# A one-core attention-plus-experts block: transposed inputs from the host, a row region per expert, a gathered return, and every engine's program written out

## The reference, cut to what matters

```python
x = x + attn(layernorm(x))        # 16 heads of 8 features, no softmax
    q, k = l2norm(x @ Wq + bq), l2norm(x @ Wk + bk);  v = x @ Wv + bv
    out  = (q @ k.T) / n ** sigmoid(m) @ v;  return out @ Wo + bo
h = layernorm(x)
    logits = h @ router_w.T       # 16 experts, top 1 for each row
    score  = sigmoid(top logit);  gate, up = split((h * score) @ gate_up[e])
    routed = (up * silu(gate)) @ down[e]
    shared = silu(h @ shared_gate.T) * (h @ shared_up.T) @ shared_down.T
return x + shared + routed
```

## Time and profile before

| | us |
|---|---|
| median of 3 runs | 277.24 (275.02 to 279.43) |
| the profiled execution, its own time | 278.11 |
| its span in the trace | 276.1 |
| busy: PE, PEld, DVE, ACT, POOL | 197.2, 169.9, 146.3, 102.3, 139.2 |
| the chain that ended last, by engine | DMA 25%, issue 20%, PE 16%, POOL 16%, DVE 15%, ACT 3% |
| of that: returning scatter (DMA and POOL) | 13% and 9% |
| of that: forward scatter (DMA and POOL) | 9% and 3% |

### The profile page before, as it was taken

How to read it: one execution, slowest core, us unless ns; L and a number is a source line. 1 busy time by engine, 2 the same in 40 slices (tenths; PEclk the granted TensorE clock), 3 DMA queues, 4 the chain that set the end, 5 groups by cost and what they waited for, 6 DMA issues and landing times.

```text
span 276.1 us, 3634 instructions
## 1 busy us (share of the span) xinstructions
PE 197.2 (71%) x1195; PEld 169.9 (62%) x1195; DVE 146.3 (53%) x368; ACT 102.3 (37%) x198; POOL 139.2 (50%) x148
## 2 busy tenths in 40 slices
PE   1786988798777699479999600999999999910000
PEld 1346666577577588468888500999999888810000
DVE  2269799999962866962333300476776333300041
ACT  3314548577574763702222100345554422200000
POOL 8004754667666130655555652014657666667360
PEclk9996899999987956959999955799999999995555
DMA  4998020250000000001111113234430111111396
GB/s 122 286 375 290 34 76 2 67 165 1 0 4 0 0 0 2 1 29 48 42 38 42 44 47 96 63 93 118 133 98 39 49 48 50 48 39 48 122 305 209
DMA packets 27906, 22.59 MB, mean 82 GB/s; under 512 B 2401, under 2 KB 24945, under 8 KB 27889
## 3 DMA queue, kind: packets, MB, share of 16 engines
q1 hardware_dynamic: 22640, 15.85, 19.9%
q0 software_dynamic: 2560, 5.26, 5.3%
q10 hardware_dynamic: 2688, 1.25, 1.6%
HBM read 11.83 MB, written 10.53 MB: 81 GB/s over the span
## 4 chain that ended last, share of the span: by engine, by line
DMA 25%; issue 20%; PE 16%; POOL 16%; DVE 15%; ACT 3%; SPq 1%; POOLq 0%; DVEq 0%; ACTq 0%
DMA y_rows<-yg,home 13%; DMA x_slots<-h_rows,pos 9%; POOL y_rows L438 9%; POOL x_slots L429 3%; DVE qkv L656 3%; DVE st L621 2%; DMA h_rows<-y_rows 2%; PE quad_banks L891 2%; DVE ss L665 2%; PE bank L975 1%; SPq L326 1%; PE bank L902 1%; PE bank L881 1%; DVE ss L669 1%; PE quad_banks L935 1%
## 5 line engine op out<-in xcount | busy, mean ns | idle before, releaser
L438 POOL DMA_INDIRECT y_rows<-yg,home x48 | 45.9, 957 | 43.6 <-DMA y_rows<-yg,home 20.5
L700 DVE TENSOR_TENSOR s_act<-quad_banks,sg_act 128x512 f32<-128x512 f32 x32 | 22.0, 691 | 44.3 <-PE bank L975 37.8
L429 POOL DMA_INDIRECT x_slots<-h_rows,pos x32 | 30.8, 963 | 22.2 <-DMA x_slots<-h_rows,pos 9.5
L531 ACT ACTIVATE sg_act<-quad_banks 128x512 f32<-128x512 f32 x32 | 18.9, 597 | 56.1 <-PE quad_banks L937 56.1
L975 PEld LDWEIGHTS bank<-sdT,s_act 128*128 128x128 f32 x256 | 35.7, 205 | 2.9
L975 PE MATMUL bank<-sdT,s_act 128*128 128x128 f32 x256 | 35.8, 288 | 0.0
L375 POOL TENSOR_TENSOR qkv<-qkv,rn 128x512 f32<-128x512 f32 x16 | 16.9, 1076 | 33.0 <-DVE rn L673 33.0
L891 PE MATMUL quad_banks<-w_c,xT 128*128 128x384 f32 x64 | 25.3, 543 | 1.7 <-ACT xT L480 1.2
L935 PE MATMUL quad_banks<-hT,sgT 128*128 128x512 f32 x32 | 16.3, 510 | 5.2 <-DVE s_act L700 5.2
L891 PEld LDWEIGHTS quad_banks<-w_c,xT 128*128 128x128 f32 x64 | 13.0, 214 | 11.1 <-issue 2.4
L1060 PE MATMUL bank<-ident,xg 128*128 128x128 f32 x48 | 7.7, 287 | 16.1 <-DMA xg<-x_slots 16.0
(11 more groups left out here) (146 smaller groups left out, 487.3 us busy)
## 6 DMA issues: line engine op xcount, KB each, us to landing
x_slots<-w_raw SPq DMA_DIRECT2D x8, 387.0 KB, 6.2
xg<-x_slots SPq DMA_DIRECT2D x12, 258.0 KB, 2.8
xres<-L_attn_x SPq DMA_DIRECT2D x8, 256.0 KB, 5.7
w_raw<-L_ffn_gate_up_proj SPq DMA_DIRECT2D x4, 512.0 KB, 3.6
h_rows<-y_rows SPq DMA_DIRECT2D x8, 256.0 KB, 5.2
out<-xres ACTq DMA_DIRECT2D x4, 256.0 KB, 4.7
out<-xres SPq DMA_DIRECT2D x4, 256.0 KB, 4.5
y_rows<-yg,home POOLq DMA_INDIRECT x48, 2.2
```

The costliest lines, as they stand in the source:

```text
L429: g.indirect_dma_start(out=x_slots, out_offset=bass.IndirectOffsetOnAxis(ap=pos[:, t:t + 1], axis=0), in_=h_rows[:, t, :], in_offset=None) ...
L438: g.indirect_dma_start(out=y_rows, out_offset=bass.IndirectOffsetOnAxis(ap=home[:, n:n + 1], axis=0), in_=yg[:, n, :], in_offset=None).the ...
L531: a.activation(sg_act[:, k % 2], pair[:, 2 * (k % 2)], ACT.Silu).then_inc(s_silu, 1)
L700: v.tensor_tensor(s_act[:, k % 2], pair[:, 2 * (k % 2) + 1], sg_act[:, k % 2], ALU.mult).then_inc(s_act_rdy, 1)
```

## The change

The whole program is written anew. What it does:

- **The host** passes x a second time in features-first form (`x_t`), stores x and the output in the layout of the SBUF tile (2 KB pieces for each partition and chunk), and passes a centering matrix, the joined q, k and v weights and biases, and every FFN weight already turned. The turns of x and of weights on PE are gone, with their copies.
- **Bias and residual** go into PSUM by PE (`attend`: an fp32r product of 512 columns, and a float32 product of the identity by 512 columns of x), and ACT copies the sum out. `add_bo` on POOL and `add_attn` on DVE are gone.
- **Router and experts' gate and up** use one plain float32 product instead of three fp32r ones; the experts' weights are no longer split. The shared products keep their split.
- **A region for each expert**: `x_slots` has 16 regions of 4096 + 128 rows. Ranks count within the expert alone, so a chunk's rows are placed as soon as the chunk is routed. Every chunk has its own `choose`, `count`, `count_before` and `place`, and the 32 scatters of POOL stand inside attention. The first 128 rows of each region are zeros, and an expert's last tile is filled up with them.
- **The score** is no longer put on the rows. The rows carry their top logit as a 129th column, and the sigmoid (silu of the logit over the logit) is applied in the expert stage, as a scale.
- **Loads**: a table of the first row of each of the 48 tiles is computed after the last chunk; SP reads it into registers and issues 48 loads of 128 rows (12 x 4).
- **Return**: each group is stored by SP in slot order (`y_slots`), and after all stores have landed POOL issues 32 indirect DMAs that gather the rows of each tile into SBUF. The adds follow chunk by chunk.
- **Every engine's list** is written out call by call, with the wait of each PE call as an argument.

The shape of the additions in the diff (the order lists and helpers cut to a few lines each):

```diff
-    x_slots = nc.dram_tensor("x_slots", (SLOTS, W), F32, kind="Internal").ap()
-    y_rows = nc.dram_tensor("y_rows", (1 + T + SLOTS, D), F32, kind="Internal").ap()
+    x_slots = nc.dram_tensor("x_slots", (E * REG, W), F32, kind="Internal").ap()
+    y_slots = nc.dram_tensor("y_slots", (SLOTS * P, D), F32, kind="Internal").ap()
...
+            def load(g):
+                first = slot_values(0, g, mybir.EngineType.SP, E * REG - P)
+                if g == 0:
+                    sp.wait_ge(zero_st, 16)
+                    for landed in scat:
+                        sp.wait_ge(landed, 16 * NT // 2)
+                for j in range(Q):
+                    sp.dma_start(xg[:, g * Q + j, :], x_slots[bass.ds(first[j], P), :]).then_inc(xg_ld[g], 16)
...
+            for stored in y_st:
+                pool.wait_ge(stored, 16 * NG // YRING)
+            pool.wait_ge(y_row_rdy, 1)
+            for t in range(NT):
+                if t >= 2:
+                    pool.wait_ge(back[t % 2], 16 * (t // 2))
+                g.indirect_dma_start(out=h_rows[:, t, 0:D], out_offset=None, in_=y_slots,
...
+            def take_y(g):
+                act.wait_ge(e_dn_mm, g + 1)
+                if g >= YRING:
+                    act.wait_ge(y_st[g % YRING], 16 * (g // YRING))
...
+            def choose(c):
+                dve.wait_ge(log_mm, c + 1)
+                logits = log_bank(c)[:, 0:Q * E].rearrange("p (t e) -> p t e", e=E)
+                top = h_rows[:, Q * c:Q * c + Q, D]
+                link(v.tensor_reduce(top, logits, AX.X, ALU.max))
+                link(v.tensor_tensor(far[:], logits, top.unsqueeze(2).broadcast_to([P, Q, E]), ALU.is_lt))
...
+            def place(c):
+                dve.wait_ge(base_mm, c + 1)
+                base = log_bank(c)[:, 128:128 + E]
+                link(v.tensor_tensor(offs[:], incl[:, c % 2], base.unsqueeze(2).broadcast_to([P, E, Q]), ALU.add))
+                link(v.tensor_tensor(offs[:], offs[:], hot[:, c], ALU.mult))
+                link(v.tensor_reduce(rank[:], offs[:].rearrange("p e t -> p t e"), AX.X, ALU.add))
+                v.tensor_tensor(pos[:, Q * c:Q * c + Q], rank[:], near[:], ALU.add).then_inc(pos_rdy, 1)
...
+                te.matmul(ps_qy[:], ones_r[:], bo_two[:].rearrange("p j d -> p (j d)"), start=True, stop=False)
+                te.matmul(ps_qy[:], ident[:], xres[:, Q * c:Q * c + Q, :].rearrange("p j d -> p (j d)"), start=False,
+                          stop=False)
...
+                    mm = te.matmul(gate_up_banks(g % 2)[:, j, :], xgT[:, g % 2, P * j:P * j + P],
+                                   gu_cols[:, bass.ds(held[g][j] * 2, F2)], start=True, stop=True)
```

More of the change, by code:

```diff
@@ L427, in _, with scatter @@
+            def scatter(t):
+                if t % Q == 0:
+                    pool.wait_ge(pos_rdy, t // Q + 1)
                 if t >= 2:
@@ new lines, in _ @@
+            scatter(0)
+            scatter(1)
+            hT_lo(1)
+            scatter(2)
+            scatter(3)
+            scale_v(4)
+            scale_q(4)
+            count(1)
+            scale_v(5)
+            scale_q(5)
+            scatter(4)
+            scatter(5)
+            scatter(6)
+            count(2)
+            scatter(7)
+            hT_lo(2)
+            scatter(8)
+            scatter(9)
+            hT_lo(3)
+            scatter(10)
+            scatter(11)
+            count(3)
@@ new lines, in _ @@
+            scale_v(6)
+            scale_q(6)
+            scatter(12)
+            scatter(13)
+            scale_v(7)
+            scatter(14)
+            scatter(15)
+            scale_q(7)
+            scatter(16)
+            scatter(17)
+            count(4)
+            hT_lo(4)
+            scatter(18)
+            scatter(19)
+            count(5)
+            hT_lo(5)
+            scatter(20)
+            scatter(21)
+            hT_lo(6)
+            scatter(22)
+            scatter(23)
@@ L706, in _ @@
+            v.memset(zeros[:], 0.0).then_inc(z_done, 1)
             dve.wait_ge(ach, 1)
@@ L854, in _ @@
-            shared(0, C1)
-            over_groups(experts, dve, lambda k: act_shared(C1, k))
-            shared(C1, NQ)
-            add_experts(NQ - 1)
+            x_stats(2)
+            x_scales(1)
+            take(0, 0)
+            x_stats(3)
+            take(0, 1)
+            bias_rows()
+            take(1, 0)
+            x_stats(4)
+            head_sums(0)
+            take(1, 1)
+            scale_mask()
+            inv_norms(0)
+            x_stats(5)
+            head_sums(1)
@@ new lines, in _ @@
+            head_sums(3)
+            inv_norms(3)
+            x1_stats(1)
+            take(4, 0)
+            choose(0)
+            mask_vk(1)
+            h_scales(1)
+            take(4, 1)
+            place(0)
+            take(5, 0)
+            head_sums(4)
+            take(5, 1)
+            inv_norms(4)
+            x1_stats(2)
+            head_sums(5)
+            choose(1)
+            inv_norms(5)
+            h_scales(2)
+            x1_stats(3)
+            place(1)
+            take(6, 0)
@@ new lines, in _ @@
+            h_scales(3)
+            mask_vk(2)
+            take(6, 1)
+            choose(2)
+            take(7, 0)
+            head_sums(6)
+            place(2)
+            x1_stats(4)
+            take(7, 1)
+            h_scales(4)
+            inv_norms(6)
+            choose(3)
+            head_sums(7)
+            x1_stats(5)
+            place(3)
+            act_shared(0)
+            inv_norms(7)
+            choose(4)
+            h_scales(5)
+            act_shared(1)
+            place(4)
@@ new lines, in _ @@
+            mask_vk(3)
+            x1_stats(6)
+            choose(5)
+            h_scales(6)
+            place(5)
+            x1_stats(7)
+            h_scales(7)
+            choose(6)
+            place(6)
+            act_shared(2)
+            choose(7)
+            place(7)
+            act_shared(3)
+            act_shared(4)
+            slot_rows()
+            act_shared(5)
+            take_table()
+            y_rows()
+            act_shared(6)
+            add_shared(0)
+            act_shared(7)
@@ L961, in gate_up_shared, with turn_h @@
-            def gate_up_shared(c, k):
-                n = c * KC + k
-                if not (isinstance(c, int) and n < 2):
-                    pe.wait_ge(s_act_rdy, n - 1)
-                h = hT[:, :, bass.ds(c * 512, 512)]
+            def turn_h(c, after=None):
+                pe.wait_ge(h_rdy, c + 1)
+                free(after)
+                for j, t in enumerate(tiles(c)):
+                    last = te.transpose(ps_hT[:, P * j:P * j + P], h_rows[:, t, 0:D], ident[:])
+                last.then_inc(hT_mm, 1)
```

1581 lines of the change are left out of this document (921 added, 660 removed).

## The result

The changed kernel takes 241.24 us (median of 4 runs, 238.15 to 242.28), where the kernel before took 277.85 on the same chip (4 runs, 275.02 to 279.43). The ratio is 0.867, with a 95% interval of 0.859 to 0.875: clearly faster. The forecast was 234.0, range 219 to 252. The profiled execution took 240.65 us, its span is 238.7. Some executions of one and the same kernel run slower, at a lower granted clock; the ratios and intervals here leave them out.

| event (us from the span's start) | predicted | measured |
|---|---|---|
| first take on DVE | 10.5 | 12.35 |
| last `place` | 98 | 112.8 |
| last forward scatter landed | 112 | 121.1 |
| rows at PE | 116 | 125.8 |
| last expert group done | 170 | 180.5 |

The account below looks back on a forecast made before the run. DVE was taken to bound attention, and POOL's indirect DMAs to keep PE waiting afterwards. Last `place` at 98, rows at PE 116, last group 170, gathers to 226 gave a span of 232.8 and 234 us, range 219 to 252.

Parts of the forecast that it names:

- Step 1: Kernel start: DVE's first take moves from 14.31 to about 10.5 us, a gain of 4 us.
- Step 2: Attention: 82.7 us of DVE work at density 0.93 takes 89 us; last `place` done at 98.
- The warning row L787: Attention: DVE instructions with two SBUF inputs held by POOL, 37 us if always, 5 us expected.
- Step 3: Forward scatters in POOL's list: 44 us taken for 32, landed at 112, rows at PE at 116.
- (a): Attention: POOL and DVE hold each other, landing waits +6 us, held instructions +10: 250 us; chance 0.17.
- Step 4: Expert stage: 3.51 us of PE for each of twelve groups, plain product 1.83; last group done at 170.
- Step 5: Return: last store landed at 174, 32 gathers 1.57 us apart to 226, span 232.8.
- (b): Return: gathers land in 3 us for 2.3, about 2.1 apart, +17 us: 251 us; chance 0.1.
- (c): SP's queue: 48 loads at 1 us each delay the stores, +12 us: 246 us; chance 0.06.
- (d): End: gathers 1.26 us apart, so PE's shared units set the end: 221 us; chance 0.13.
- (e): Return: slower than before, 283 us, if gathers wait serially by twos at 3.1 us apart; chance 0.02.
- Its own signs: Right: DVE over 18 of 20 us busy, 20 to 90; wrong: DVE instructions of 0.9 beside POOL's, DVE under 80%.

Follow-up runs that it names:

- late_scatter: The kernel after, with the 32 forward scatters moved behind the last count in POOL's list: 274.44 us, ratio 0.987.
- engines_cleared: The kernel after, with the first four shared products moved behind the last route and throwaway PE work in attention instead: 242.54 us, ratio 0.878.
- gather_four: The kernel after, with four returning gathers in flight instead of two: 232.69 us, ratio 0.838.
- shared_behind: The kernel after, with shared gate-and-up products 11 to 13 and down products 11 and 12 moved behind the last expert group: 240.39 us, ratio 0.868.
- four_behind: The kernel after, with four gathers and four scatters in flight and shared products 11 to 13 behind the last expert group: 234.79 us, ratio 0.846.
- all_three: four_behind, with the experts' gate and up product also taken once from rounded rows and weights: 227.55 us, ratio 0.824.
- one_product_b: The kernel after, with the experts' gate and up product taken once from rounded rows and weights, rounded by POOL: 235.33 us, ratio 0.847.

## Why the prediction was right, and where it was off

**The direction and the bulk of the size** were right for the stated reason. Taking the scatters out of attention again cost 33 us in `late_scatter`, and the two stages of the earlier trace rows in which PE waited for POOL are filled. That the sum came within 3% is in part luck: 14.8 us too few up to the last `place` met 5.7 too many for the scatters and 5.3 too many for the return. A slip of 0.2 us in the last addition (226, 0.8 and 5.8 are 232.6) changes nothing.

**Step 1, start.** The first take came at 12.35, a gain of 2 us for 4. DVE's list has statistics of three chunks and two scales ahead of the take, and the second of them waited for x to land (DVE, kernel after):

```profile
9.75 0.87 DVE L694 BATCH_NORM_STATS2 st<-xres 128x6 f32<-128x128 f32 x4 [3.04 <-DMA xres<-L_attn_x]
...
12.35 1.11 DVE L731 SCALAR_TENSOR_TENSOR qkv<-quad_banks,rs,b_qkv 128x384 f32<-128x384 f32 x2
```

From 9.75 to 12.35 DVE hardly paused, so the landing of x and the statistics set the start.

**Step 2, the last `place` at 98, is the step that failed in size:** 112.8. The split of DVE's own time shows where. Busy time of DVE in the kernel after, to the 4.01 us wait and from there to the last `place`:

```profile
0.00:87.90 87.90, 76.01 (x246) 0.98 0.42 123
87.90:112.90 25.00, 13.35 (x51) 0.73 0.10 32
```

The sum had 82.7 us of work; it was 76.01 + 13.35 = 89.4, 6.7 more. The ten small instructions took 25.4 us for the 17.2 assumed (the records overlap a little, so their sum is more than they add to the 89.4): unheld they are 0.16 to 0.30 us, 18.5 for 80, and the rest is L765, L780 and L782 being held. Idle time ahead of 87.9 was 11.9 us; by the prediction's 4 us and its density, for the work that it had ahead of the tail, it would have been 9.2: 2.7 more. And the tail of 25.0 us would by the density of 0.93 and the 5 us for the last chunk's chain have been 13.35/0.93 + 5 = 19.4: 5.6 more. 6.7 + 2.7 + 5.6 = 15.0, the whole miss. A density read from the full pipeline was used to its very end, where the pipeline drains: there is one chain and not eight. Some 2.5 of the tail's 25 us are shared work on PE at the lower clock (`engines_cleared`); the rest of its idle time is the waits of the chain.

**The warning row L787 was read rightly, its price was too low.** A held instruction ends with the tensor instruction of POOL that stands beside it (DVE and POOL of the kernel after):

```profile
56.26 1.69 DVE L765 SCALAR_TENSOR_TENSOR far<-far,place_of 128x64 f32<-128x64 f32 x1
...
72.82 1.53 DVE L717 SCALAR_TENSOR_TENSOR nm<-mv,rs 128x4 f32<-128x4 f32 x1
```

```profile
55.74 2.11 POOL L308 TENSOR_TENSOR qkv<-qkv,rn 128x512 f32<-128x512 f32 x2
...
73.03 1.29 POOL L318 TENSOR_TENSOR hT<-hT_full,hT 128x512 fp32r<-128x512 f32 x1
```

The first ends at 57.95 and POOL's scales at 57.85, the second at 74.35 and POOL's low part at 74.32. L765, L780 and L782 lost (0.684 - 0.226) x 8 + (0.508 - 0.225) x 8 + (0.281 - 0.162) x 8 = 6.9 us, for the 5 assumed. L717 lost another 3.1, but that isn't new: the kernel before has the same instruction, held as long, inside the 74.0 us that the sum started from:

```profile
L642 DVE SCALAR_TENSOR_TENSOR nm<-mv,rs 128x4 f32<-128x4 f32 x8 | 4.0, 497 | 0.3
```

Nor did the 5 us stand in the 0.93, as the prediction says: going from 0.956 to 0.93 adds 82.7/0.93 - 82.7/0.956 = 2.4 us. Without scatters in attention (`late_scatter`) DVE's work to the last `place` was 84.4, 5 us less. Other timing of POOL's list changes which instructions meet; no single cause of these 5 us was isolated. The Trainium skill, SBUF — State Buffer, section Who interferes with whom, says that DVE's two-port copies starve the descriptors of GpSimd's DMAs. No run here can show it: DVE's list beside these scatters is products, statistics, reductions and reciprocals, with hardly a copy. The scatters took 975 ns in the median for 957, and 959 in `gather_four` with the same attention.

**Step 3.** The scatters weren't late: four of them followed the last `place` in 5.8 us, and the last landed 8.3 us behind it, where the prediction had 14. What was left of rival (a), landing waits, was 4.4 us. Of the 14.8 us, 5.7 were given back here.

**Step 4, experts.** From rows at PE to the last group 54.7 us for 54 predicted, with PE busy as assumed. The plain product took 1.73 us for each group (1.83 assumed; rows of the chain that ended last):

```profile
153.13 1.73 PE quad_banks L1221 x8
155.30 0.89 PE bank L1240 x8
```

Against the 1.52 of the twelve split products that is 1.14 times. The Trainium skill's four passes against three would have been 1.33 times (FP8 and Floating Point Precision, section TensorE Precision Notes): for the time, the measurement decides. It doesn't refute the count of passes. The profile shows two instructions for each product, of 1.73/8 = 0.216 us, and each split product of the same width took 1.52/12 = 0.127 us, so two of the one kind cost as much as 3.4 of the other.

**Step 5, return.** 1.516 apart for the 1.57 taken; landing to the end 4.0 us for 6.9. So 174 to 232.8 was predicted as 58.8 us and took 53.5: 5.3 us too many, which hid a third of step 2's miss. On the span the miss is thus +14.8 at the last `place`, -5.7 in the scatters, three times +0.7 (to the rows at PE, to the last group, to the first gather) and -5.3 at the return: 5.9.

**Rivals.** (a) came in part: 4.4 us of landing waits for its 6, and 6.9 us of held instructions for its 10; the forecast had counted 5 of the latter. (b) fell: landings were 2.6 us. (c) fell: the 48 loads took 29.3 us, 0.61 each, and no copy waited for a store. (d) didn't come in after, but is what ends `shared_behind`, `four_behind` and `all_three`. (e) was far off.

**Its own signs.** The gathers' spacing and the products of 0.216 us came as it said. The last `place` (112.8) and the last scatter (118.6) lay outside 95 to 101 and 106 to 114. Of the signs of being wrong, the first came: small DVE instructions of 0.9 us and more beside POOL's. And DVE, over 18 of 20 us busy from 40 to 80, fell to 13.4 and 13.8 from 80 to 120, under 80%: there the chain of latencies did set the pace.

## What to carry to other kernels

A density read from a full pipeline prices the work up to where it drains; the last chunk's chain is to be added up step by step, with each engine's copy and wait. Work that seems to be in the way at such a place can be what keeps TensorE's granted clock up: with it gone the last `place` came 4.2 us later, with throwaway work in its stead 2.4 us earlier. Where it goes matters as much: moved ahead of a small step that others wait for (here the table of rows), it cost some 5 us more. And where DMAs go out one by one with waits for an earlier landing, the number in flight is worth an early try: two more semaphores gave 8 us, more than any edit of the work, until PE's own work set the end.

## What the runs showed that was not expected

- With four shared products less, TensorE was granted 0.50 (1.2 GHz) for all of 80 to 100 us, where it had 0.87 with them (0.83 to 1.00 in the six runs with unchanged attention) and 1.00 with throwaway products in their place. The residual product of two 512-column halves took 2.08 us at the lower level and 1.12 at the upper.
- Gathers from DRAM into SBUF land in 2.5 us with four in flight as with two (2.6): POOL's 0.94 us and a gap of 0.30 are then the whole price.
- A single product from rounded operands takes 4 instructions for each group in place of 8, and 0.73 to 0.89 us where PE's timeline has 1.89 to 1.99 for the plain one.
- DVE instructions of 4 columns (0.16 us) took up to 1.5 us, and one of 32 columns (0.19 us) took 3.02 beside POOL's rounding of weights in `one_product_b`. The held ones read here ended within 0.1 us of a tensor instruction of POOL. The kernel before has such holds too.
